# Householder steps with row b summed in PSUM, QL sweeps spread over ten steps, and v.Bv by a scalar-tensor-tensor instruction

## The chip, the cores and the metric

The kernel runs on 1 core of one Trainium2 chip. The metric is the device time of one execution in microseconds (us). Before the change it is 1569.76 us, the median of 3 runs (1568.9 to 1571.31).

## The reference

The input is x (64, 128, 128) and a symmetric normalised adjacency matrix adj (128, 128). Four graph layers follow one another, each as x = x + layer(relu(layernorm(x))). The first layer is spectral: it needs the eigenvectors U of the normalised Laplacian of adj. The others are a two-layer mixing network with batch norm, a two-layer graph convolution with four short LSTMs, and masked attention. The change touches only the eigendecomposition:

```python
deg = jnp.sum(A, axis=0) + jnp.sum(A, axis=1) - jnp.diagonal(A)
d_inv_sqrt = jnp.where(deg > 0, jax.lax.rsqrt(deg), 0.0)
L = jnp.diag(deg) - A
L_norm = d_inv_sqrt[:, None] * L * d_inv_sqrt[None, :]
_, U = jnp.linalg.eigh(L_norm)
agg = jnp.einsum('mn,bnd->bmd', U.T, features)
```

All of it is float32. The signs of the eigenvectors count too, because a relu stands between U.T and U.

## The kernel before, in words

The eigendecomposition comes first and nothing of the four layers runs beside it. All engines run hand-written queues with semaphores between them; `Chain` gives the semaphore by which an engine waits for its own earlier instruction. The stages are:

1. **Tridiagonalisation** (`hh_step`, 126 steps, K=N-2). Step k makes a Householder reflector v from row k of B and updates B by two outer products. Rows are kept as 1 x n tiles on one partition, with n = 127-k columns for the part that is still alive. On VectorE (DVE) a step goes: scalars of the norm (L317 to L323), x0 (L326), Bv (L330), the sum v.Bv (L333, by the custom instruction of the helper in L259, followed by a read of its accumulator), x1 (L335), w (L337), the next row x (L341), the sign of its first element (L310, L311), and B = B + P[3] (L348). ScalarE (ACT) squares and sums the row (L652), takes the root (L654), copies the column out of PSUM (L656), copies row b out of PSUM (L658) and scales v (L660). TensorE (PE) has five float32 products in a step, each run as two passes: the column (L700), row b = row k+1 of B by a column of the identity (L702, after the update of B in L348), the product x.B (L704), and the two outer products (L707, L709). PE issues in program order.
2. **Leaf work beside it.** From step 16 on, implicit QL sweeps run on the top 16 x 16 block of the tridiagonal matrix, to fix the sign of one eigenvector. GpSimd (POOL) does most of it, DVE does the divisions, scans and reductions in short pieces (`leaf_at`), and ACT one square root in a sweep (`leaf_root_of`). A step of the tridiagonalisation has two spots for DVE's pieces: the even one after L326 and before L330, the odd one after L311 and before L348. A sweep takes SPOTS=16 spots, so eight steps. DVE's pieces have 13 instructions in a sweep, at phases 0, 2, 3, 5, 6 and 8. There are 16 sweeps. Steps 16 to 125 hold 220 spots; the rest runs in the next stage.
3. **Sturm counts** (`count_below`, two passes of 63 iterations on DVE, each ending in L448). Every odd iteration of pass 0 has a leaf spot. ACT and PE count signs behind DVE; before that they work through the transposes of the LSTM weights, which are loaded one after the other.
4. **Twisted factorisation** (L486 to L495): 127 iterations on DVE alone, of two reciprocals and two multiply-adds. Then come the eigenvector's entries and sign, the back-transformation and two refinements.
5. The four layers.

## Time and profile before

| what | value |
|---|---|
| median of 3 runs | 1569.76 us |
| profiled execution, its own time | 1570.16 us |
| its span | 1568.5 us |
| tridiagonalisation | 24.7 to 410.9 us |
| Sturm pass 0 / pass 1 | from 427.4 us / from 498.5 us |
| twisted factorisation | 549.3 to 620 us |
| busy share of the span | PE 72%, DVE 67%, ACT 44%, POOL 16% |
| chain that ended last, by engine | PE 50%, DVE 35%, issue 7%, ACT 4% |

Times in the rows are us from the span's start. A row of the timeline has the start, the duration, the engine, the line, the operation, what it writes and reads, shapes and a count; in square brackets stands how long the engine was idle before it and who ended that. L690 is the helper that records nearly all products of this part, and L259 the helper of the custom sum, so these are told apart by tiles. PE's durations include the way through the array: products with single-column weights can start one behind the other before the first one's row ends.

### The profile page before, as it was taken

The numbers are of one execution on the slowest core, as the hardware profiler recorded it, in microseconds if no ns is written. First come the engines' busy times: TensorE is split into PE (matmuls) and PEld (weight loads), VectorE is DVE, ScalarE is ACT, GpSimd is POOL, SyncE is SP. The second block draws the span as 40 slices with busy tenths as digits, with TensorE's granted clock in tenths as the row PEclk, the third lists the DMA queues.
The fourth block names the chain that finished last, engine by engine and source line by source line (L and its number), as shares of the span: only waits on it lengthen the run. The fifth ranks groups of instructions, "written<-read, shape, count | busy, mean of one in ns | idle before, by whom it ended". The sixth has DMA issues, their size and how long they took to land.

```text
span 1568.5 us, 21564 instructions
## 1 busy us (share of the span) xinstructions
PE 1124.1 (72%) x5260; PEld 714.5 (46%) x5260; DVE 1045.5 (67%) x4156; ACT 690.6 (44%) x1760; POOL 253.9 (16%) x900
## 2 busy tenths in 40 slices
PE   3777777776542300448787668999999998589998
PEld 2445555555421200335453356444455443367777
DVE  7777788777889999755576754444343354664766
ACT  2334444444231200024365457675554545365665
POOL 4045555666450000000000000000010020000000
PEclk9999999999975555559898679999999999597999
DMA  4000000000100000000000000000000000000001
GB/s 138 1 1 1 1 1 1 1 1 2 29 21 1 1 0 0 1 0 0 0 0 0 0 0 0 0 0 0 0 0 0 0 0 0 0 15 13 27 20 34
DMA packets 16654, 12.30 MB, mean 8 GB/s; under 512 B 665, under 2 KB 14530, under 8 KB 16578
## 3 DMA queue, kind: packets, MB, share of 16 engines
q1 hardware_dynamic: 16578, 11.49, 2.6%
q8 instruction: 22, 0.36, 0.1%
q14 instruction: 54, 0.44, 0.1%
HBM read 7.23 MB, written 4.19 MB: 7 GB/s over the span
## 4 chain that ended last, share of the span: by engine, by line
PE 50%; DVE 35%; issue 7%; ACT 4%; DVEq 1%; DMA 1%; POOL 1%; ACTq 0%; POOLq 0%
PE P L1343 30%; PE P L690 9%; PE P L1492 4%; DVE B L348 2%; DVE arena L330 2%; DVE arena L444 2%; DVE arena L495 1%; DVE arena L493 1%; DVE scal L320 1%; DVE bst_all L909 1%; ACT hb L1154 1%; DVE arena L448 1%; DVE arena L259 1%; DVE arena L337 1%; PE P L1485 1%
## 5 line engine op out<-in xcount | busy, mean ns | idle before, releaser
L1343 PE MATMUL P<-arena,WT 128*128 (+2 forms) x792 | 329.1, 579 | 3.9 <-ACT L1242 2.9
L1343 PEld LDWEIGHTS P<-arena,WT 128*128 128x128 f32 x792 | 151.8, 192 | 181.1 <-issue 167.3
L690 PE MATMUL P<-arena 1*128 1x127 f32 (+62 forms) x504 | 166.1, 434 | 87.1 <-DVE arena L330 48.6
L1255 ACT ACTIVATE arena<-P,bl 128x512 f32<-128x512 f32 (+1 forms) x252 | 153.3, 636 | 139.5 <-PE P L1343 130.7
L690 PEld LDWEIGHTS P<-arena 1*128 1x128 f32 x504 | 124.1, 307 | 142.4 <-DVE arena L330 112.8
L898 POOL COPY arena<-arena 128x512 f32<-128x512 f32 x16 | 21.5, 1386 | 783.0 <-DVE arena L1075 691.2
L1064 DVE TENSOR_TENSOR arena<-arena 128x512 f32<-128x512 f32 (+1 forms) x36 | 22.0, 610 | 137.4 <-ACT arena L1255 137.4
L652 ACT ACTIVATE arena<-arena 1x127 f32<-1x127 f32 (+62 forms) x126 | 32.2, 256 | 167.5 <-DVE arena L341 157.2
L1154 ACT ACTIVATE hb<-xN,nmr,rsd 128x128 f32 (+1 forms) x192 | 78.5, 481 | 34.9 <-PE P L1343 28.1
L690 PE MATMUL P<-arena,Ib 128*128 128x46 bf16 (+1 forms) x318 | 34.4, 268 | 60.9 <-ACT arena L679 60.4
L195 POOL TENSOR_SCALAR lf<-lf 1x1 f32<-1x1 f32 x210 | 73.3, 349 | 21.9
L1492 PEld LDWEIGHTS P<-arena 128*128 128x128 f32 x512 | 66.6, 200 | 21.5 <-issue 13.2
L1492 PE MATMUL P<-arena 128*128 128x33 f32 x512 | 69.1, 281 | 7.2 <-ACT arena L1300 7.2
L690 PEld LDWEIGHTS P<-I,arena 1*128 1x128 f32 x252 | 66.4, 321 | 4.1 <-DVE arena L305 4.0
L690 PE MATMUL P<-I,arena 1*128 1x1 f32 x252 | 65.0, 325 | 3.2 <-DVE arena L305 3.2
L690 PE MATMUL P<-leaf,ones 1*128 1x1 f32 x2 | 0.6, 342 | 82.5 <-DVE leaf L533 82.5
L690 PE MATMUL P<-B,I 128*1 128x128 f32 (+62 forms) x252 | 47.8, 286 | 11.6 <-DVE B L348 7.6
L690 PEld LDWEIGHTS P<-arena,Ib 128*128 128x128 bf16 x318 | 18.9, 116 | 76.6 <-ACT arena L679 64.1
L690 PE MATMUL P<-B,xcol 128*1 128x128 f32 (+62 forms) x252 | 50.9, 299 | 2.5
L1115 DVE TENSOR_REDUCE mx<-P 128x4 f32<-128x512 f32 x64 | 43.7, 683 | 12.1 <-PE P L1478 12.1
L1062 DVE TENSOR_TENSOR arena<-arena 128x512 f32<-128x512 f32 (+1 forms) x36 | 25.9, 718 | 37.4 <-ACT arena L1255 37.3
L660 ACT ACTIVATE arena<-arena,scal 1x128 f32<-1x128 f32 (+62 forms) x126 | 43.6, 346 | 14.1 <-DVE arena L326 11.4
(477 smaller groups left out, 2451.2 us busy)
## 6 DMA issues: line engine op xcount, KB each, us to landing
out_dram<-xN SPq DMA_DIRECT2D x16, 256.0 KB, 2.3
Wn<-in_L_gnn_Wih_dram SPq DMA_DIRECT2D x4, 256.0 KB, 2.9
Wn<-in_L_gnn_Whh_dram SPq DMA_DIRECT2D x4, 256.0 KB, 2.8
Wqkv<-in_L_gnn_W_dram SPq DMA_DIRECT2D x1, 192.0 KB, 3.6
W1n<-in_L_gnn_W_dram SPq DMA_DIRECT2D x1, 128.0 KB, 4.1
W2n<-in_L_gnn_W_dram SPq DMA_DIRECT2D x1, 128.0 KB, 4.0
Wg<-in_L_gnn_Wg_dram SPq DMA_DIRECT2D x2, 64.0 KB, 3.6
adj<-in_adj_dram SPq DMA_DIRECT2D x1, 64.0 KB, 1.8
```

Of the source, the lines that this page charges most:

```text
L195: l.mark(ts(leaf_p[:,i+1:i+2],leaf_p[:,i:i+1],leaf_x[:,i:i+1],leaf_na[:,i-2:i-1],ALU.mult,ALU.add))
L330: stt(Bv_row[:,k:N],b_row[:,k:N],scal[:,1:2],P[1][0:1,k:N],ALU.mult,ALU.add).then_inc(ev('Bv'),1)
L348: tt(B[:,k+1:N],B[:,k+1:N],P[3][:,k+1:N],ALU.add).then_inc(ev('B_updated'),1)
L444: b=c.mark(tt(seq_d[:,0:2*W],slotS(q),D2[:,i*2*W:(i+1)*2*W],ALU.mult))
L652: a.activation(square_row[:,k+1:N],u[:,k+1:N],ACT.Square,accum_out=scal[:,7:8]).then_inc(ev('column_norm2'),1)
L660: a.activation(v_row[:,k:N],u[:,k:N],ACT.Copy,scale=scal[:,10:11]).then_inc(ev('v_scaled'),1)
L690: def mm(o,l,r,start=True,stop=True): return t.matmul(o,lhsT=l,rhs=r,start=start,stop=stop)
L1115: v.tensor_reduce(s.mx[:,h*4:h*4+4],S3,AX.X,ALU.max).then_inc(ev('attention_max'),1)
L1154: i=a.activation(s.hb[u][:,b*N:(b+1)*N],s.xN[:,bass.ds((2*it+u)*C+b*N,N)],ACT.Relu,bias=s.nmr[:,bass.ds(col,1)],scale=s.rsd[:,bass.ds(col,1)])
L1255: act(s.gt[u][gate][:,0:cols],P[4*u+gate][:,0:cols],f,bias=s.bl[:,4*(p-1)+gate:4*(p-1)+gate+1]).then_inc(ev('lstm_gates'),1)
L1343: def mm(o,l,r,start=True,stop=True,**k): return t.matmul(o,lhsT=l,rhs=r,start=start,stop=stop,**k)
L1492: i=t.matmul(O[:,o:o+33],lhsT=s.pT[h%2][:,b*N:(b+1)*N],rhs=s.vx[u][:,b,h,:],start=True,stop=True)
```

## The change

Three things change.

- **Row b.** It is no longer read from the updated B. In step k, once row b has been copied out, PE starts a sum in P[0] with row k+2 of the B that is not yet updated, adds Bv[k+2] times v, and in the next step adds v[k+2] times w. So P[0] has the updated row without a wait on L348. PE has seven products in a step instead of five; the two new ones have a single element as weights.
- **Leaf sweeps.** A sweep takes 20 spots (ten steps) instead of 16. Seven of DVE's 13 instructions in a sweep go to POOL (multiplications, additions, one comparison, the radicand); six are left, at phases 0, 2 (two), 6, 7 and 10. The 16 sweeps now end in the twisted factorisation: leaf spots stand in both Sturm passes and in iterations up to i=53 of the factorisation. ACT's roots move with them.
- **v.Bv** is a scalar-tensor-tensor with the factor 1.0 and an accumulator output.

```diff
-SPOTS=16
+SPOTS=20
         def rotations(sweep):
-            eng.wait_ge(ev('leaf_from_vector'),5*sweep-1)
+            eng.wait_ge(ev('leaf_from_vector'),5*sweep)
...
-        def new_offdiagonals(sweep):
-            eng.wait_ge(ev('leaf_from_vector'),5*sweep)
-            l(tt(rows(300,20),rows(200,20),rows(240,20),ALU.mult))
-            l(tt(rows(300,20),rows(300,20),rows(142,100),ALU.mult))
-            l(tt(leaf_4e2,row(300,15),row(320,15),ALU.mult))
-            l(ts(leaf_n4,leaf_4e2,-1.0,None,ALU.mult))
+        def new_block(sweep):
+            eng.wait_ge(ev('leaf_from_vector'),5*sweep+1)
+            l(tt(leaf_gamma[:,0:16],leaf_q,leaf_rz,ALU.mult))
+            l.mark(tt(rows(300,20),rows(200,20),rows(240,20),ALU.mult))
+            l.mark(tt(leaf_sums16,leaf_gamma[:,0:16],leaf_gamma[:,1:17],ALU.subtract))
+            l.wait(l.n-1)
+            l.mark(tt(rows(300,20),rows(300,20),rows(142,100),ALU.mult))
+            l.wait(l.n-1)
+            l.mark(ts(leaf_sums16,leaf_sums16,0.5,None,ALU.mult))
+            l.wait(l.n-1)
+            l.mark(tt(leaf_4e2,row(300,15),row(320,15),ALU.mult))
+            l.wait(l.n-1)
+            l.mark(tt(leaf_d[:,0:16],leaf_sums16,leaf_d[:,1:17],ALU.add))
+            l.wait(l.n-1)
+            l.mark(ts(leaf_n4,leaf_4e2,-1.0,None,ALU.mult))
+            l.wait(l.n-1)
+            l(ts(leaf_dd,leaf_d[:,0:15],4*EPS*EPS,None,ALU.mult))
+            l(tt(leaf_dd,leaf_dd,leaf_d[:,1:16],ALU.mult))
         def alive(sweep):
-            if sweep: eng.wait_ge(ev('leaf_from_vector'),5*sweep+1)
...
         def shift(sweep):
             eng.wait_ge(ev('leaf_from_vector'),5*sweep+2)
+            l(ts(leaf_pick,section[0:1,0:15],leaf_idx,None,ALU.is_equal))
             tt(rows(60,20,3),rows(0,20,3),leaf_pick.unsqueeze(1).broadcast_to([1,3,15]),ALU.mult).then_inc(ev('leaf_from_gpsimd'),1)
-            eng.wait_ge(ev('leaf_radicand'),sweep+1)
+            eng.wait_ge(ev('leaf_from_vector'),5*sweep+3)
+            ts(leaf_radicand,leaf_sums[:,0:1],leaf_sums[:,0:1],leaf_sums[:,2:3],ALU.mult,ALU.subtract).then_inc(ev('leaf_radicand'),1)
...
         def shifted(sweep):
-            eng.wait_ge(ev('leaf_from_vector'),5*sweep+3)
+            eng.wait_ge(ev('leaf_from_vector'),5*sweep+4)
+            l(ts(leaf_d[:,16:17],leaf_rden,leaf_sums[:,2:3],leaf_sums[:,1:2],ALU.mult,ALU.add))
...
-            vp=c.mark(ttr(unused_row[:,k+1:N],u[:,k+1:N],Bv_row[:,k+1:N],scal[:,5:6]))
+            vp=c.mark(stt(unused_row[:,k+1:N],u[:,k+1:N],1.0,Bv_row[:,k+1:N],ALU.mult,ALU.mult,accum_out=scal[:,5:6]))
...
-                c(v.reciprocal(leaf_rz,leaf_z[:,0:16]))
-                tt(leaf_gamma[:,0:16],leaf_q,leaf_rz,ALU.mult).then_inc(ev('leaf_from_vector'),1)
-            if phase==3 and sweep:
-                v.wait_ge(ev('leaf_from_vector'),5*sweep)
-                c(tt(leaf_sums16,leaf_gamma[:,0:16],leaf_gamma[:,1:17],ALU.subtract))
-                c(stt(leaf_d[:,0:16],leaf_sums16,0.5,leaf_d[:,1:17],ALU.mult,ALU.add))
-                stt(leaf_dd,leaf_d[:,0:15],4*EPS*EPS,leaf_d[:,1:16],ALU.mult,ALU.mult).then_inc(ev('leaf_from_vector'),1)
-            if phase==5:
+                v.reciprocal(leaf_rz,leaf_z[:,0:16]).then_inc(ev('leaf_from_vector'),1)
+            if phase==6:
                 v.wait_ge(ev('leaf_from_gpsimd'),5*sweep+1)
-                c(v.tensor_reduce(leaf_idx,leaf_hot,AX.X,ALU.max))
-                ts(leaf_pick,section[0:1,0:15],leaf_idx,None,ALU.is_equal).then_inc(ev('leaf_from_vector'),1)
-            if phase==6:
+                v.tensor_reduce(leaf_idx,leaf_hot,AX.X,ALU.max).then_inc(ev('leaf_from_vector'),1)
+            if phase==7:
                 v.wait_ge(ev('leaf_from_gpsimd'),5*sweep+2)
-                c(v.tensor_reduce(leaf_sums,rows(60,20,3),AX.X,ALU.add))
-                stt(leaf_radicand,leaf_sums[:,0:1],leaf_sums[:,0:1],leaf_sums[:,2:3],ALU.mult,ALU.subtract).then_inc(ev('leaf_radicand'),1)
-            if phase==8:
+                v.tensor_reduce(leaf_sums,rows(60,20,3),AX.X,ALU.add).then_inc(ev('leaf_from_vector'),1)
+            if phase==10:
                 v.wait_ge(ev('leaf_from_gpsimd'),5*sweep+3)
-                c(v.reciprocal(leaf_rden,leaf_den))
-                stt(leaf_d[:,16:17],leaf_rden,leaf_sums[:,2:3],leaf_sums[:,1:2],ALU.mult,ALU.add).then_inc(ev('leaf_from_vector'),1)
+                v.reciprocal(leaf_rden,leaf_den).then_inc(ev('leaf_from_vector'),1)
...
-                if pass_==0 and i%2 and HH_SPOTS+i//2<=SPOTS*(SWEEPS-1)+8: leaf_at(HH_SPOTS+i//2)
+                if i%2: leaf_at(HH_SPOTS+HN//2*pass_+i//2)
...
+            if i%2 and HH_SPOTS+HN+i//2<=SPOTS*(SWEEPS-1)+10: leaf_at(HH_SPOTS+HN+i//2)
             c.wait(f)
             f=c.mark(v.reciprocal(inv_down[:,i-1:i],D_down[:,i-1:i]))
...
-            if sweep>=0 and phase==6: leaf_root_of(sweep)
+            if sweep>=0 and phase==8: leaf_root_of(sweep)
...
-                i=2*(SPOTS*sweep+6-HH_SPOTS)+1
-                if h<HALVES and i>0 and i//(SEG//2)==h: leaf_root_of(sweep)
+                root_spot=SPOTS*sweep+8-HH_SPOTS
+                if root_spot>=0 and root_spot//(SEG//4)==h: leaf_root_of(sweep)
...
+        for sweep in range(SWEEPS):
+            if SPOTS*sweep+8-HH_SPOTS>=HN: leaf_root_of(sweep)
...
             mm(P[4][:,0:1],reflector(k),I[0:1,0:1]).then_inc(ev('column_psum'),1)
+            if k: mm(P[0][0:1,k:N],v_row[:,k+1:k+2],w_row[:,k:N],start=False).then_inc(ev('row_b_psum'),1)
             t.wait_ge(ev('B_updated'),k+1)
-            mm(P[0][0:1,k:N],I[:,k+1:k+2],B[:,k:N]).then_inc(ev('row_b_psum'),1)
+            if not k: mm(P[0][0:1,0:N],I[:,1:2],B[:,:]).then_inc(ev('row_b_psum'),1)
             t.wait_ge(ev('column'),k+1)
             mm(P[1][0:1,k:N],xcol[:,:],B[:,k:N]).then_inc(ev('row_xB'),1)
+            t.wait_ge(ev('row_b'),k+1)
+            if k+1<K: mm(P[0][0:1,k+1:N],I[:,k+2:k+3],B[:,k+1:N],stop=False)
             t.wait_ge(ev('Bv'),k+1)
             t.wait_ge(ev('v_scaled'),k+1)
             mm(P[3][:,k+1:N],Bv_row[:,:],v_row[:,k+1:N],stop=False)
+            if k+1<K: mm(P[0][0:1,k+1:N],Bv_row[:,k+2:k+3],v_row[:,k+1:N],start=False,stop=False)
             t.wait_ge(ev('w_row'),k+1)
             mm(P[3][:,k+1:N],v_row[:,:],w_row[:,k+1:N],start=False).then_inc(ev('outer_products'),1)
```

## Rows read from the trace of the kernel before

**Rows 1.** Tridiagonalisation: length; PE, PEld, DVE, ACT, POOL busy (x); PEclk; DMA, GB/s.

```profile
24.70:410.20 385.50, 285.03 (x1252) 206.90 (x1253) 302.59 (x1931) 160.44 (x764) 187.10 (x755) 1.00 0.00 1
```

**Rows 2.** Groups by line, tridiagonalisation: xcount | busy, mean ns | idle before.

```profile
L330 DVE SCALAR_TENSOR_TENSOR arena<-arena,scal,P 1x127 f32<-1x127 f32 (+62 forms) x125 | 32.7, 261 | 11.0 <-PE P L690 9.8
```

**Rows 3.** Timeline, early step, all engines.

```profile
31.05 0.79 PE L690 MATMUL P<-arena 1*128 1x125 f32 x2 [0.50 <-DVE arena L330]
32.00 0.78 PE L690 MATMUL P<-arena 1*128 1x125 f32 x2 [0.16 <-DVE arena L337]
33.23 0.58 PE L690 MATMUL P<-B,I 128*1 128x125 f32 x2 [0.21 <-DVE B L348]
33.60 0.62 PE L690 MATMUL P<-B,xcol 128*1 128x125 f32 x2
33.74 0.15 DVE L326 TENSOR_TENSOR arena<-arena,scal 1x1 f32<-1x1 f32 x1
34.33 0.33 DVE L330 SCALAR_TENSOR_TENSOR arena<-arena,scal,P 1x125 f32<-1x125 f32 x1 [0.43 <-PE P L690]
```

**Rows 4.** Timeline of DVE, a step in the middle.

```profile
207.81 0.28 DVE L330 SCALAR_TENSOR_TENSOR arena<-arena,scal,P 1x74 f32<-1x74 f32 x1
208.23 0.22 DVE L259 CUSTOM_DVE_ANT_0 arena<-arena 1x73 f32<-1x73 f32 x1
208.39 0.07 DVE L259 DVE_READ_ACCUMULATOR2_ANT scal<- 1x1 f32 x1
208.39 0.28 DVE L335 SCALAR_TENSOR_TENSOR arena<-arena 1x72 f32<-1x72 f32 x1
208.59 0.28 DVE L337 SCALAR_TENSOR_TENSOR arena<-arena,scal 1x73 f32<-1x73 f32 x1
208.97 0.28 DVE L341 SCALAR_TENSOR_TENSOR arena<-arena 1x72 f32<-1x72 f32 x1
```

**Rows 5.** Groups by line: scalar-tensor-tensor on one element, immediate or pointer.

```profile
L311 DVE SCALAR_TENSOR_TENSOR scal<-arena 1x1 f32<-1x1 f32 x125 | 17.2, 138 | 0.0
L386 DVE SCALAR_TENSOR_TENSOR lf<-lf 1x1 f32<-1x1 f32 x14 | 2.9, 206 | 0.5
```

**Rows 6.** Timeline, L341 alone, a middle and a late sweep.

```profile
236.34 0.27 DVE L341 SCALAR_TENSOR_TENSOR arena<-arena 1x63 f32<-1x63 f32 x1
257.30 0.27 DVE L341 SCALAR_TENSOR_TENSOR arena<-arena 1x56 f32<-1x56 f32 x1
260.09 0.28 DVE L341 SCALAR_TENSOR_TENSOR arena<-arena 1x55 f32<-1x55 f32 x1
...
351.21 0.24 DVE L341 SCALAR_TENSOR_TENSOR arena<-arena 1x23 f32<-1x23 f32 x1
353.74 0.23 DVE L341 SCALAR_TENSOR_TENSOR arena<-arena 1x22 f32<-1x22 f32 x1
356.81 0.23 DVE L341 SCALAR_TENSOR_TENSOR arena<-arena 1x21 f32<-1x21 f32 x1
370.38 0.22 DVE L341 SCALAR_TENSOR_TENSOR arena<-arena 1x16 f32<-1x16 f32 x1
372.87 0.22 DVE L341 SCALAR_TENSOR_TENSOR arena<-arena 1x15 f32<-1x15 f32 x1
```

**Rows 7.** One line each: min/median/max ns, first to last start.

```profile
L448 DVE TENSOR_TENSOR arena<-arena x63: 178/246/290, 427.4 to 480.4; 128x92 f32<-128x92 f32 x63
L448 DVE TENSOR_TENSOR arena<-arena x63: 245/247/256, 498.5 to 544.3; 128x92 f32<-128x92 f32 x63
L493 DVE TENSOR_SCALAR arena<-neg_off,arena x127: 262/265/273, 549.3 to 619.9; 128x1 f32<-128x1 f32 x127
```

**Rows 8.** Timeline of Sturm pass 0: ACT, then DVE.

```profile
447.37 0.48 ACT L670 ACTIVATE arena<-P 128x368 bf16<-128x368 f32 x1
448.67 0.28 ACT L648 ACTIVATE lf<-lf 1x1 f32<-1x1 f32 x1
449.76 0.15 DVE L385 RECIPROCAL lf<-lf 1x1 f32<-1x1 f32 x1 [2.31 <-POOL lf L226]
```

More of the change, by code:

```diff
@@ L246, in _ @@
                 rotations(sweep)
-                new_offdiagonals(sweep)
+                new_block(sweep)
             alive(sweep)
```

## The prediction

> **What bounds the kernel now.** I read the page first, for the stages: the change touches only the eigendecomposition, and the layers behind it start when it ends, so a microsecond saved there is one of the time. Then the busy times by stage, then the groups by line, and then the timeline of single steps. In the tridiagonalisation DVE is busy 302.59 of 385.50 us and PE 285.03, at the full clock of 1.00 [rows 1]. Neither is full: a step is a ring of short instructions that hand over to each other, and the reader is to look for who starts last at each handover.
>
> Three handovers matter. (1) Bv (L330) waits for the product x.B. In an early step that product starts at 33.60, right behind the product for row b, which starts at 33.23, as soon as B is updated; L330 starts at 34.33 after 0.43 us idle that PE ended [rows 3]. Over all steps L330's engine is idle 11.0 us before it, 9.8 of them by PE [rows 2]; in the middle step at 74 columns its row shows no idle time [rows 4]. (2) From L330 to L341 DVE works in its own order: L330 starts at 207.81, the custom sum at 208.23, x1 at 208.39, w at 208.59, the next row at 208.97 [rows 4]. Each is on the ring. (3) DVE's leaf pieces stand in the same queue ahead of L330 or of L348. What they cost is the excess of a sweep's steps over free ones. In the middle, the eight steps from 236.34 to 260.09 take 23.75 us; a free step there takes 2.79 (257.30 to 260.09), and as steps shrink with the columns the mean over the eight would be about 2.84, so 22.7: excess 1.05. Late, 351.21 to 372.87 is 21.66 us against eight times about 2.52 (the free one at the end is 2.49): excess 1.5. The piece with scan, reciprocal and product is the dearest: 3.07 for its step (353.74 to 356.81) against 2.52, while the lone reciprocal's step takes 2.53 [rows 6].
>
> **Row b.** The product of 125 columns leaves its place between the update of B and x.B, so x.B can start up to 0.37 us earlier (33.23 for 33.60) [rows 3]. The 0.43 us that DVE is idle leave room for it. The third part of the new sum now stands before x.B, but right behind the column's product, where PE waits for L348 and for the copied column anyway: it is one more product of the same column count with a gap ahead of x.B, so I cost it at nothing; if that cover is gone, it takes back up to the same 0.37. The gain goes to zero where L330 no longer waits for PE, at some 62 to 74 columns [rows 4]. A triangle of 0.36 us over 62 steps is 11 us, which agrees with the 9.8 us of idle time plus what lies hidden in leaf steps [rows 2].
>
> PE has two more products. Row k+2 of the old B goes between x.B's end and the outer products, where PE waits about half a microsecond for Bv; nothing. The product Bv[k+2] times v goes between the two outer products. In the early step these start at 31.05 and 32.00, and the first one's row ends at 31.84 [rows 3]. The inserted one occupies PE about as long as the gap between two single-weight products, 0.37 us at 125 columns; part of it overlaps the first one's tail. I take a delay of the second outer product of 0.05 to 0.1 us for the first 27 steps and none later: 2 us. That delay is on the path, since L348 follows the second outer product and DVE's scalars stand behind L348 in the queue. The bounds for this term are 0 and 0.2 us in every step, as below. Row b nets 11 - 2 = **9 us**.
>
> **Leaf pieces.** Before, the tridiagonalisation holds 220/16 = 13.75 sweeps; at 1.05 each (early ones less, late ones up to 1.5) 14.4 us. After, 11 sweeps with six instructions each. From the late sweep: the lone reciprocal costs about 0; scan plus reciprocal without the product 0.55 less 0.2, so 0.35; a reduction before L330 0.1, a reduction before L348 (where DVE waits for PE) nothing, the reciprocal of one element 0.05: 0.5 a sweep, 5.5 us. Gain **9 us**. What it needs is that POOL keeps up: it is busy 187.10 us for 13.75 sweeps [rows 1], 13.6 a sweep; seven more instructions of 0.2 to 0.3 us make about 15.5, with waits perhaps 19, in ten steps of at least 24.9 us (2.49 each [rows 6]).
>
> The rest of the leaf work moves to later stages. Pass 0 takes 53.0 us (427.4 to 480.4), pass 1, without leaf pieces, 45.8 [rows 7]. Of the 7.2 us, 2.3 are one stall for ACT's root [rows 8]; 4.9 are 26 instructions, so 0.19 each. After, pass 0 has 12 instructions (2.3 us), pass 1 nine (1.7), the twisted factorisation nine (1.7; it is DVE alone, 0.56 us an iteration [rows 7]). The stall gets longer: ACT can take the root only when it has done the weights' copies and the first sign groups. In the new order the root stands behind the group at 447.37 instead of the one before 448.67, so it starts at about 447.8, and DVE goes on as long after it as now, 1.09 us (448.67 to 449.76 [rows 8]): at 448.9. But DVE now wants it at i=21 instead of i=25. It is there at 427.4 + 20 x 0.74 (45.8/62) + 0.9 for four pieces = 443.1. Stall 5.8 for 2.3. Sum behind the tridiagonalisation: 2.3 + 1.7 + 1.7 + 5.8 - 7.2 = **4.3 us lost**.
>
> **v.Bv.** The trace of before has no such instruction with an accumulator. The custom one starts 0.14 us after L330's end (207.81 + 0.28 to 208.23), where L341 starts 0.10 after L337's (208.59 + 0.28 to 208.97): 0.04 that may go. From the custom one to x1 are 0.16 us, with the accumulator's read (0.07) beside x1. A plain scalar-tensor-tensor of the same length holds the queue 0.20 (208.39 to 208.59) [rows 4], but it takes its scalar by a pointer; with an immediate it is 0.07 shorter on one element (138 against 206 ns) [rows 5]. So from 0.07 shorter (0.04 + 0.16 - 0.13) to 0.07 longer (0.20 + 0.07 - 0.16 - 0.04): -9 to +9 us over 126 steps. Both forms near it have the immediate's price, but the read may cost; I take -0.02 a step, **2.5 us gained**.
>
> A page speaks against this part. In the rows, a plain scalar-tensor-tensor takes 0.33 us for 125 columns and 0.28 for 74 [rows 3, 4], 1.0 ns a column, so it is not halved by two float32 inputs in SBUF. The Trainium skill's page "Vector Engine (DVE) Microarchitecture Reference", section "Points that are easy to get wrong", says that this form with two non-bf16 SBUF sources halves throughput, since no port is left for the accumulator's readback. The rows contradict it without an accumulator; with one no row here shows it. By that rule the sum would come out as in rival 3.
>
> **Sum.** 1570.16 (the profiled execution's own time, 1.7 above its span and 0.4 above the median of the runs) - 9 - 9 - 2.5 + 4.3 = **1554 us**.
>
> **Rivals.**
> 1. *PE's queue becomes the bound (slower).* The inserted product delays the second outer product in every step, and with it L348, the scalars and the next column. For it: the early outer products leave only 0.16 us idle between them [rows 3]. Against it: with fewer columns the inserted product shrinks at 3 ns a column while DVE's chain from Bv to w shrinks at half of that. It decides from 0.13 us a step (16/126). At 0.2 us, a fourth of the early outer product's 0.79 [rows 3], the cost is 25 us: 1554 + 25 = 1579. Chance 9%.
> 2. *Row b brings nothing*, since the third part takes the place of the product removed. 1554 + 9 = 1563. For it: same column count, still ahead of x.B in an in-order queue. Against it: the wait for L348 between them. Chance 11%.
> 3. *The accumulator form is dear.* Without halving, +9 for -2.5: 1565.5, chance 12%. With 1.0 ns more for each of 64 columns on average, another 8 us: 1573.5, chance 4%.
> 4. *POOL or the root holds DVE up*, about 1 us in each of 16 sweeps: 1570. For it: the stall at 449.76. Chance 5%. That the change doesn't do what it says has no weight of its own: the removed instructions are plain in the diff.
>
> The forecast has the remaining 59%. Its own range is 1547 to 1560. The range for 8 in 10 takes in the term v.Bv from -9 to +9, a leaf gain of 12, and rivals 2 and 3 without halving: 1544 to 1567. A difference under 0.2% (3 us) is no change for a measurement of this kernel. Faster is the forecast, rival 2, and rival 3 without halving: 0.82. Rival 4 is the same, with a part of rival 3: 0.06. Slower: rival 1 and the halving: 0.12.
>
> **What would show it.** In the early step L330 should start some 0.3 us earlier after the update of B, with x.B starting right behind the update; steps of 60 columns and less without leaf pieces should be as long as now, but for v.Bv. The tridiagonalisation should end 20 us earlier. A sweep's excess should be 0.5 us in ten steps. The reciprocal of phase 10 in pass 0 should wait about 6 us for POOL. The prediction is wrong if the second outer product starts more than 0.1 us after w in middle steps, if x1 starts later than 0.2 us after the sum, or if a reduction waits for POOL in most sweeps.

## The result, and the profile after

The changed kernel takes 1573.7 us (median of 12 runs, 1571.33 to 1590.61) against 1568.93 us before (12 runs, 1567.56 to 1571.31). The ratio is 1.0048, with a 95% interval of 1.0028 to 1.0069: about 5 us slower, where 1554 us was forecast. Of the 12 runs of the changed kernel eight lie between 1571.3 and 1574.2 us, three between 1581.4 and 1582.4, and one at 1590.6; the profile below is of the one at 1581.65.

The busy times by stage of the changed kernel, columns as in [rows 1]: the tridiagonalisation, from its end to the eigenvectors, and the layers behind.

```profile
24.70:421.90 397.20, 350.44 (x1751) 220.82 (x1749) 288.85 (x1819) 161.55 (x761) 176.06 (x705) 1.00 0.01 1
421.90:704.40 282.50, 74.32 (x484) 46.39 (x483) 243.24 (x1233) 36.15 (x81) 92.53 (x294) 0.57 0.03 7
704.40:1579.80 875.40, 758.54 (x3512) 458.89 (x3512) 480.48 (x949) 492.21 (x910) 21.18 (x16) 0.92 0.02 5
```

The first row answers to [rows 1]. DVE is busy 288.85 us for 302.59: the leaf work did leave. But the stage is 11.7 us longer (397.20 for 385.50), and PE has 499 more matmul records and 65 us more busy time. The second stage is 2.9 us longer (279.6 before). The third is 3.3 us shorter (878.70 before), though the change touches nothing in it.

Where the 11.7 us sit is in DVE's groups by line of the same stage (L344 is Bv, before L330; L362 the update of B, before L348; L347 v.Bv):

```profile
L344 DVE SCALAR_TENSOR_TENSOR arena<-arena,scal,P 1x127 f32<-1x127 f32 (+62 forms) x125 | 32.7, 262 | 10.7 <-PE P L698 3.9 <-DVE wide L368 0.2
L362 DVE TENSOR_TENSOR B<-B,P 128x127 f32<-128x127 f32 (+62 forms) x125 | 27.8, 223 | 54.8 <-PE P L698 54.8
L347 DVE SCALAR_TENSOR_TENSOR arena<-arena 1x126 f32<-1x126 f32 (+62 forms) x125 | 27.0, 216 | 14.3 <-DVE arena L344 0.5
L347 DVE DVE_READ_ACCUMULATOR arena<-arena 1x1 f32 x125 | 8.8, 71 | 0.0
```

Before Bv, the idle time put down to PE fell from 9.8 us [rows 2] to 3.9, but all idle time there only from 11.0 to 10.7: the short gaps, put down to nobody, have grown. Before the update of B, DVE is idle 54.8 us, all of it until PE's outer products; the same line of before reads:

```profile
L348 DVE TENSOR_TENSOR B<-B,P 128x127 f32<-128x127 f32 (+62 forms) x125 | 27.5, 220 | 21.9 <-PE P L690 21.7
```

So 33 us of new waiting stand at one handover. With row b as before and the other two parts in place (e1 below) the wait there is 28.1 us: 6 of the 33 come from the work taken off DVE, 27 from row b. An early step of the changed kernel shows how; it answers to [rows 3] and the steps around it (start, us, engine, line, operation, idle time before):

```profile
35.42 0.33 DVE L351 SCALAR_TENSOR_TENSOR arena<-arena,scal 1x124 f32<-1x124 f32 x1
35.60 0.08 PEld L698 LDWEIGHTS P<-arena 1*1 1x1 f32 x2 [0.22 <-issue]
36.10 0.50 PEld L698 LDWEIGHTS P<-arena 1*128 1x128 f32 x2 [0.42 <-DVE arena L351]
...
36.99 0.28 DVE L362 TENSOR_TENSOR B<-B,P 128x124 f32<-128x124 f32 x1 [0.56 <-PE P L698]
...
37.04 0.57 PE L698 MATMUL P<-arena 1*1 1x124 f32 x2
...
37.54 0.57 PE L698 MATMUL P<-B,xcol 128*1 128x124 f32 x2
...
38.22 0.33 DVE L344 SCALAR_TENSOR_TENSOR arena<-arena,scal,P 1x124 f32<-1x124 f32 x1 [0.22 <-PE P L698]
```

w (L351) is ready at 35.75, but the second outer product's weights load only at 36.10: 0.35 us later. Between the two outer products stands the single-element product, whose weights load at 35.60. In a middle step it is the same:

```profile
205.98 0.28 DVE L351 SCALAR_TENSOR_TENSOR arena<-arena,scal 1x75 f32<-1x75 f32 x1
...
206.54 0.50 PEld L698 LDWEIGHTS P<-arena 1*128 1x128 f32 x2 [0.25 <-DVE arena L351]
...
207.35 0.23 DVE L362 TENSOR_TENSOR B<-B,P 128x75 f32<-128x75 f32 x1 [0.45 <-PE P L698]
...
208.42 0.28 DVE L344 SCALAR_TENSOR_TENSOR arena<-arena,scal,P 1x75 f32<-1x75 f32 x1
...
208.81 0.24 DVE L347 SCALAR_TENSOR_TENSOR arena<-arena 1x74 f32<-1x74 f32 x1
...
208.99 0.07 DVE L347 DVE_READ_ACCUMULATOR arena<-arena 1x1 f32 x1
208.99 0.28 DVE L349 SCALAR_TENSOR_TENSOR arena<-arena 1x73 f32<-1x73 f32 x1
```

w ends at 206.26 and the weights load at 206.54, 0.28 us later.

For the rest it helps to cut each step in three, by the starts on DVE: Bv to w, w to the update of B, the update to the next Bv. Summed over all steps, from each kernel's trace (us):

| kernel | Bv to w | w to update | update to Bv: first 45 steps | next 40 | last 40 |
|---|---|---|---|---|---|
| before | 97.7 | 144.2 | 59.3 | 44.6 | 41.8 |
| after | 93.7 | **169.6** | 52.5 | 42.8 | 40.5 |
| after, row b as before (e1) | 92.8 | 142.9 | 58.2 | 41.1 | 38.1 |
| leaf part alone (e3) | 97.2 | 142.5 | 58.3 | 41.1 | 38.1 |
| v.Bv alone (e4) | 93.8 | 144.5 | 59.2 | 44.6 | 41.9 |
| row b alone (e2) | 98.5 | 164.5 | 54.1 | 45.6 | 43.1 |

### The profile page after: what moved, and what is told of

It is laid out like the page before. It is cut to its first block, busy times and chain, and to the rows that moved or that the text cites. A ratio compares the mean times of both kernels' runs of the same rounds, so it can differ in the third digit from the quotient of the medians.

```text
span 1579.8 us, 22704 instructions
## 1 busy us (share of the span) xinstructions
PE 1188.3 (75%) x5760; PEld 728.6 (46%) x5760; DVE 1032.8 (65%) x4048; ACT 692.8 (44%) x1760; POOL 306.4 (19%) x1038
## 4 chain that ended last, share of the span: by engine, by line
PE 57%; DVE 29%; issue 6%; ACT 5%; DVEq 1%; DMA 1%; ACTq 0%; POOL 0%; POOLq 0%
PE P L1355 29%; PE P L698 17%; PE P L1504 3%; DVE arena L449 2%; DVE bst_all L921 2%; DVE arena L499 1%; DVE arena L501 1%; DVE scal L334 1%; ACT hb L1166 1%; ACT arena L666 1%; DVE arena L453 1%; DVE arena L344 1%; DVE arena L447 1%; PE P L1497 1%; PE P L1463 1%
## 5 line engine op out<-in xcount | busy, mean ns | idle before, releaser
L698 PE MATMUL P<-arena 1*128 1x127 f32 (+62 forms) x1004 | 245.2, 356 | 36.6 <-ACT arena L666 24.3
L1267 ACT ACTIVATE arena<-P,bl 128x512 f32<-128x512 f32 (+1 forms) x252 | 153.5, 636 | 137.4 <-PE P L1355 130.0
L698 PEld LDWEIGHTS P<-arena 1*128 1x128 f32 x1004 | 145.0, 191 | 115.0 <-DVE arena L344 69.5
L1166 ACT ACTIVATE hb<-xN,nmr,rsd 128x128 f32 (+1 forms) x192 | 78.5, 481 | 34.8 <-PE P L1355 28.1
L195 POOL TENSOR_SCALAR lf<-lf 1x1 f32<-1x1 f32 x210 | 85.6, 408 | 21.9
L362 DVE TENSOR_TENSOR B<-B,P 128x127 f32<-128x127 f32 (+62 forms) x126 | 28.0, 222 | 55.4 <-PE P L698 55.4
L698 PE MATMUL P<-B,xcol 128*1 128x128 f32 (+62 forms) x252 | 47.7, 286 | 10.1 <-ACT xcol L662 6.6
```

The costliest lines, as they stand in the source:

```text
L195: l.mark(ts(leaf_p[:,i+1:i+2],leaf_p[:,i:i+1],leaf_x[:,i:i+1],leaf_na[:,i-2:i-1],ALU.mult,ALU.add))
L362: tt(B[:,k+1:N],B[:,k+1:N],P[3][:,k+1:N],ALU.add).then_inc(ev('B_updated'),1)
L698: def mm(o,l,r,start=True,stop=True): return t.matmul(o,lhsT=l,rhs=r,start=start,stop=stop)
L1166: i=a.activation(s.hb[u][:,b*N:(b+1)*N],s.xN[:,bass.ds((2*it+u)*C+b*N,N)],ACT.Relu,bias=s.nmr[:,bass.ds(col,1)],scale=s.rsd[:,bass.ds(col,1)])
L1267: act(s.gt[u][gate][:,0:cols],P[4*u+gate][:,0:cols],f,bias=s.bl[:,4*(p-1)+gate:4*(p-1)+gate+1]).then_inc(ev('lstm_gates'),1)
```

## The experiments

Theory D (delay): the product put between the outer products holds back the second one in every step. Its rival in the tridiagonalisation: what is lost lies in the leaf part or the accumulator form. Theory P (position): what the layers take depends on when they start.

**e1: the change without row b.**

```diff
-            if k: mm(P[0][0:1,k:N],v_row[:,k+1:k+2],w_row[:,k:N],start=False).then_inc(ev('row_b_psum'),1)
...
+            mm(P[0][0:1,k:N],I[:,k+1:k+2],B[:,k:N]).then_inc(ev('row_b_psum'),1)
...
-            if k+1<K: mm(P[0][0:1,k+1:N],I[:,k+2:k+3],B[:,k+1:N],stop=False)
...
-            if k+1<K: mm(P[0][0:1,k+1:N],Bv_row[:,k+2:k+3],v_row[:,k+1:N],start=False,stop=False)
```

> The changed kernel with the products of row b as before (five a step). Theory D (the two single-element products delay PE): steps of 75 columns without leaf pieces fall from 3.2 us to 2.95, the tridiagonalisation ends before 402 us, and the time is 1559 to 1564, some 12 us under the changed kernel. Rival L (the leaf sweeps over ten steps cost what was lost, through POOL): steps stay near 3.2 us and the time stays at 1570 or more.

Measured: 1547.05 us (4 runs, 1546.19 to 1547.84), ratio to before 0.9868 [0.9851, 0.9884]. The row-b part alone turns a gain of 1.3% into a loss of 0.5%. It is also 12 us below the expected range, and that mixes two things. Against the changed kernel, whose layers take 867.4 us in its second profile (e12) and e1's 865.4, nearly all of the difference is in the tridiagonalisation: 26.1 us, where some 12 were expected. Against before, the layers are 13.3 us shorter (865.4 for 878.7), which no expectation had. The busy times of its tridiagonalisation and the group of the update of B:

```profile
24.80:395.90 371.10, 280.96 (x1253) 205.54 (x1253) 287.30 (x1819) 158.39 (x761) 176.90 (x705) 1.00 0.00 1
```

```profile
L362 DVE TENSOR_TENSOR B<-B,P 128x127 f32<-128x127 f32 (+62 forms) x125 | 27.8, 222 | 28.1 <-PE P L698 26.5
```

The stage is 26.1 us shorter than after's, and the wait before the update 26.7 us shorter (54.8 to 28.1): in sum the whole difference is that handover. The gain and the loss from the update to Bv nearly cancel (135.8 us in after, 137.4 in e1). One middle step of e1 for the 206.54 above:

```profile
195.18 0.28 DVE L351 SCALAR_TENSOR_TENSOR arena<-arena,scal 1x76 f32<-1x76 f32 x1
...
195.51 0.49 PEld L698 LDWEIGHTS P<-arena 1*128 1x128 f32 x2 [0.23 <-DVE arena L351]
...
196.33 0.23 DVE L362 TENSOR_TENSOR B<-B,P 128x76 f32<-128x76 f32 x1 [0.24 <-PE P L698]
```

The weights load 0.05 us after w's end (195.46), not 0.28, and the update starts 1.15 us after w's start, not 1.37.

**e2: row b alone, on the kernel before.** The same four products as above, put into before.

```diff
+            if k: mm(P[0][0:1,k:N],v_row[:,k+1:k+2],w_row[:,k:N],start=False).then_inc(ev('row_b_psum'),1)
...
-            mm(P[0][0:1,k:N],I[:,k+1:k+2],B[:,k:N]).then_inc(ev('row_b_psum'),1)
+            if not k: mm(P[0][0:1,0:N],I[:,1:2],B[:,:]).then_inc(ev('row_b_psum'),1)
...
+            if k+1<K: mm(P[0][0:1,k+1:N],I[:,k+2:k+3],B[:,k+1:N],stop=False)
...
+            if k+1<K: mm(P[0][0:1,k+1:N],Bv_row[:,k+2:k+3],v_row[:,k+1:N],start=False,stop=False)
```

> The kernel before with only the new sum of row b. Theory D: the second outer product starts 0.3 us later after w than before in steps of every length, steps of 75 columns take about 3.2 us, and the time is 1577 to 1583. Rival L: steps up to 62 columns gain up to 0.3 us and the time is about 1560.

Measured: 1587.05 us (1585.75 to 1601.54), ratio 1.0147 [1.0095, 1.0199]. That is 4 us above the expected range. Its tridiagonalisation takes 403.8 us, 18.3 more than before. On top of the leaf part and the accumulator form it costs 26.1 (397.2 against 371.1). From w to the update it adds 20.3 us to before and 26.7 to e1: where before has leaf pieces ahead of L348, DVE comes late anyway and PE's delay is hidden (from w to the update 1.37 us before and 1.38 in e2, at 102 columns), and after has fewer of those.

**e3: the leaf part alone** (e1 with v.Bv by the custom instruction).

```diff
-            vp=c.mark(stt(unused_row[:,k+1:N],u[:,k+1:N],1.0,Bv_row[:,k+1:N],ALU.mult,ALU.mult,accum_out=scal[:,5:6]))
+            vp=c.mark(ttr(unused_row[:,k+1:N],u[:,k+1:N],Bv_row[:,k+1:N],scal[:,5:6]))
```

> The kernel before with only the leaf sweeps over ten steps. Theory D: a sweep's excess over free steps falls from 1.05 us to 0.5, 9 us are gained in the tridiagonalisation and 3 to 4 lost behind it: 1562 to 1565. Rival L: 1572 or more, with DVE's reductions waiting for POOL.

Measured: 1550.75 us (1549.97 to 1558.97), 0.9907 [0.9878, 0.9935]. Tridiagonalisation 375.1 us, 10.4 shorter. The time is 11 us below the expected range, by the layers (865.3 us for 878.7).

**e4: v.Bv alone, on the kernel before.**

```diff
-            vp=c.mark(ttr(unused_row[:,k+1:N],u[:,k+1:N],Bv_row[:,k+1:N],scal[:,5:6]))
+            vp=c.mark(stt(unused_row[:,k+1:N],u[:,k+1:N],1.0,Bv_row[:,k+1:N],ALU.mult,ALU.mult,accum_out=scal[:,5:6]))
```

> The kernel before with only v.Bv by the scalar-tensor-tensor instruction with accumulator. From the changed kernel's trace it starts 0.03 us sooner after Bv and x1 starts 0.02 us later after it: 0 to 2 us gained, 1567 to 1569. The rival that it is dear: 1575 or more.

Measured: 1564.88 us (10 runs, 1563.78 to 1566.64), 0.9977 [0.9968, 0.9987]. Tridiagonalisation 382.1 us, 3.4 shorter; of the table's three segments only Bv to w changed (97.7 to 93.8). The expectation, 0 to 2 us gained, was too low: it had x1 start later behind the sum, and it doesn't (0.16 us in the mean over steps in both). The rival that the accumulator form is dear is out.

**e5 and e6: an idle product between the outer products.** Both are e1 with one product whose result nobody reads. Its moving side has one column, so it streams next to nothing; its weights have one element in e5 and 128 in e6, as the outer products' have. If any further instruction costs, both are slow; if the change of the weights' shape does, only e5.

```diff
+            mm(P[6][0:1,0:1],Bv_row[:,k+1:k+2],v_row[:,k+1:k+2])
```

```diff
+            mm(P[6][:,0:1],Bv_row[:,:],v_row[:,k+1:k+2])
```

> The changed kernel with row b as before, and one idle product added between the outer products: weights of one element and one moving column, into an unused bank; its result is not used. Theory D (what costs is the change of the weights' shape, on which PE waits until the product before has left the array): the second outer product starts 0.25 to 0.3 us later after w in steps of all lengths, and the time is 25 to 35 us over the same kernel without it (1547): 1572 to 1582. Rival Q (what costs is the columns that the inserted products stream): one column costs nothing, 1547 to 1550.

> As the last one, but the idle product has all 128 elements of the row as weights, the outer products' own shape, and again one moving column. Theory D: no wait for the array, but two loads of 128 columns, 0.2 us each; they fit between the outer products where those are long (75 columns and more), and delay the second one by up to 0.4 us at 17 columns: 1555 to 1565, with early steps unchanged. Rival Q: 1547 to 1550.

Measured: e5 1558.47 us (10 runs, 1556.5 to 1573.34), 0.9942 [0.9913, 0.9971], tridiagonalisation 382.2; e6 1573.76 (1570.64 to 1586.76), 1.0027 [0.9992, 1.0061], tridiagonalisation 395.5. Both expectations were missed: e5 lies between theory D's 1572 to 1582 and rival Q's 1547 to 1550, and e6, meant as the cheap one, is the dearer. Late steps say why; DVE's next row (L355) at 17 and 16 columns in e1, e5 and e6:

```profile
355.52 0.22 DVE L355 SCALAR_TENSOR_TENSOR arena<-arena 1x17 f32<-1x17 f32 x1
358.01 0.22 DVE L355 SCALAR_TENSOR_TENSOR arena<-arena 1x16 f32<-1x16 f32 x1
```

```profile
363.42 0.22 DVE L355 SCALAR_TENSOR_TENSOR arena<-arena 1x17 f32<-1x17 f32 x1
366.13 0.22 DVE L355 SCALAR_TENSOR_TENSOR arena<-arena 1x16 f32<-1x16 f32 x1
```

```profile
373.19 0.22 DVE L355 SCALAR_TENSOR_TENSOR arena<-arena 1x17 f32<-1x17 f32 x1
376.10 0.22 DVE L355 SCALAR_TENSOR_TENSOR arena<-arena 1x16 f32<-1x16 f32 x1
```

A step takes 2.49, 2.71 and 2.91 us. In early steps neither costs anything: w to update sums to 55.2, 55.3 and 55.9 us over the first 45 steps, since the idle product is through before w is there. So a change of shape alone is free where there is time for it; in after the inserted product streams its 124 columns as well. Late, the gap between the first outer product and w closes, and both delay the second: 42.8, 50.2 and 58.3 us over the last 41. In e6's late steps the loads of 128 weights follow each other at 0.21 us a pass, whatever is moved, so the wide product is the dearer one there. An inserted product thus costs in two ways, by its loads and by its shape, and this pair doesn't separate them. e9 does.

**e9: row b with wide weights.** The three products take all elements from k+2 on (126-k of them) as weights, and use one row of the result.

```diff
...
-            if k+1<K: mm(P[0][0:1,k+1:N],Bv_row[:,k+2:k+3],v_row[:,k+1:N],start=False,stop=False)
+            if k+1<K: mm(P[0][0:K-k,k+1:N],Bv_row[:,k+2:N],v_row[:,k+1:N],start=False,stop=False)
```

> The changed kernel with wide weights in the sum: the products take all elements from k+2 on, 126-k of them, as weights, so rows k+2 to 127 of the update stand in P[0] and row k+2 is the first. While there are over 64 of them the shape is that of the outer products. Theory D: until step 62 steps are 0.1 to 0.2 us shorter than in the changed kernel, and from there they are as long as in it: 1560 to 1570. Rival Q: no difference, 1573.

Measured: 1564.88 us (10 runs, 1563.37 to 1573.33), 0.9972 [0.9948, 0.9996], against 1.0048 for the changed kernel: the same sums in the same order, with larger loads, and 9 us less. w to update takes 56.0 us over the first 45 steps, against 66.8 in after and 55.2 in e1. Then, within one step, the gain is gone; the next rows of e9 from 66 down to 63 columns, which is also the number of the inserted product's weights in that step:

```profile
221.13 0.27 DVE L355 SCALAR_TENSOR_TENSOR arena<-arena 1x66 f32<-1x66 f32 x1
224.07 0.27 DVE L355 SCALAR_TENSOR_TENSOR arena<-arena 1x65 f32<-1x65 f32 x1
227.01 0.27 DVE L355 SCALAR_TENSOR_TENSOR arena<-arena 1x64 f32<-1x64 f32 x1
230.27 0.27 DVE L355 SCALAR_TENSOR_TENSOR arena<-arena 1x63 f32<-1x63 f32 x1
```

2.94 us a step twice, then 3.26, of which about 0.2 are a leaf piece that e1 has at the same place (2.84, then 3.03). From w to the update no leaf piece mixes in; here it is in the steps with 65 and with 64 weights:

```profile
223.70 0.27 DVE L351 SCALAR_TENSOR_TENSOR arena<-arena,scal 1x66 f32<-1x66 f32 x1
...
224.81 0.23 DVE L362 TENSOR_TENSOR B<-B,P 128x66 f32<-128x66 f32 x1 [0.23 <-PE P L698]
...
226.63 0.28 DVE L351 SCALAR_TENSOR_TENSOR arena<-arena,scal 1x65 f32<-1x65 f32 x1
...
228.07 0.22 DVE L362 TENSOR_TENSOR B<-B,P 128x65 f32<-128x65 f32 x1 [0.52 <-PE P L698]
```

1.11 us, then 1.44; e1 has 1.12 in both. The single records of PE show where it goes. With 65 weights the inserted product's load starts 0.11 us after the second pass of the first outer product, and the next outer product's load 0.11 us after the inserted one's second pass. With 64 it is 0.35 and 0.24 us. One column fewer can't cost that by its size: from 64 weights on, PE treats the inserted product as another shape than the 128 of the outer products. This is a threshold, not a slope, and it is what tells the change of shape from the loads. At 32 weights there is no second jump (0.33 us at 33 and at 32).

The Trainium skill's page "TensorEngine Tiling (Array Packing)", section "Key Properties", says: "Changing tiling mode (not just tile) drains the TensorE". The jump of e9 at 64 weights agrees with it, if a product of 64 weights or fewer runs in another mode than one of 128; no run here shows the mode itself. What the traces do show is the drain: at all 375 places in after where a product with one weight stands next to an outer or a column's product with 128, the load starts no sooner than 0.07 us before the recorded end of the product before it, while behind a product of the same shape it starts 0.2 to 0.4 us before that end.

**e7: no single-element product.** It leaves out both products that carry the update, so row b is that of the B before the update: of the three products the one that reads I and B keeps its place behind x.B.

```diff
-            if k: mm(P[0][0:1,k:N],v_row[:,k+1:k+2],w_row[:,k:N],start=False).then_inc(ev('row_b_psum'),1)
...
-            if k+1<K: mm(P[0][0:1,k+1:N],Bv_row[:,k+2:k+3],v_row[:,k+1:N],start=False,stop=False)
```

> The changed kernel without both single-element products: row b is the row of B before the update (its output is wrong by that). It shows what taking the update out of row b's path is worth by itself. The prediction put that at 11 us, mostly in steps over 75 columns: against 1547 without the sum of row b, 1536 to 1540, with steps of 124 columns at 3.3 us and steps of 75 and less as in the kernel with row b as before. If theory D is wrong and the early product with the old B costs, it stays over 1550.

Measured: 1547.64 us (4 runs, 1543.71 to 1561.87), 0.9866 [0.9793, 0.9938]; tridiagonalisation 368.3 us. That is 2.7 us below e1, where some 10 were expected. Update to Bv in e7 is 51.5 us over the first 45 steps, against 58.2 in e1: 6.7 gained. Then it is 42.9 and 40.5 against 41.1 and 38.1: 4.2 lost. An early step of e7 shows the limit of the gain:

```profile
35.56 0.28 DVE L362 TENSOR_TENSOR B<-B,P 128x124 f32<-128x124 f32 x1 [0.27 <-PE P L698]
36.04 0.57 PE L698 MATMUL P<-B,xcol 128*1 128x124 f32 x2 [0.35 <-ACT xcol L662]
...
36.72 0.33 DVE L344 SCALAR_TENSOR_TENSOR arena<-arena,scal,P 1x124 f32<-1x124 f32 x1
```

Update to Bv is 1.16 us here, 1.23 in after (36.99 to 38.22), 1.43 in e1. With row b out of the way x.B waits for ACT's copy of the column: at most 0.27 us are to be had, not 0.37. The loss in later steps is a slower start of x.B: its weights load 0.11 us after the column's copy ends when PE has nothing before it (348.27 to 348.38 in e7), and 0.06 us when the row-b product has just run (349.00 to 349.06 in e1). Why was not tried.

**e8: the root earlier.** e1, with ACT's root of pass 0 put ahead of the last copy of the LSTM weights instead of behind a sign group.

```diff
-                if root_spot>=0 and root_spot//(SEG//4)==h: leaf_root_of(sweep)
+                if sweep>HH_SPOTS//SPOTS and root_spot//(SEG//4)==h: leaf_root_of(sweep)
...
+        if q==7: before_last()
```

> The changed kernel with row b as before (1547) and ACT's root for the sweep that starts in Sturm pass 0 taken before the last copy of the LSTM weights instead of behind the first sign groups. From the stall of the reciprocal of phase 10, 5 to 6 us come off pass 0: 1541 to 1543, if the clock in the layers stays as it is. If the sign groups set the end of the pass instead, 1546 to 1547.

Measured: 1541.43 us (4 runs, 1541.08 to 1541.85), 0.9824 [0.9808, 0.9841]. The changed kernel's reciprocal of phase 10 in pass 0, then the same one in e8 with its root:

```profile
459.94 0.15 DVE L391 RECIPROCAL lf<-lf 1x1 f32<-1x1 f32 x1 [5.69 <-POOL lf L239]
```

```profile
425.49 0.28 ACT L654 ACTIVATE lf<-lf 1x1 f32<-1x1 f32 x1
...
428.38 0.14 DVE L391 RECIPROCAL lf<-lf 1x1 f32<-1x1 f32 x1
```

The stall of 5.69 us (forecast 5.8) is gone, and pass 0 takes 47.5 us for e1's 53.9, as expected.

**e10: before, with 3 us more ahead of the layers.** One DVE instruction on a scratch area between pass 1 and the twisted factorisation.

```diff
+        c(tt(arena2[:,0:2900],arena2[:,0:2900],arena2[:,2900:5800],ALU.max))
```

> The kernel before with one idle DVE instruction of about 3 us between Sturm pass 1 and the twisted factorisation. All kernels so far with the leaf sweeps over ten steps are 3 us longer between the tridiagonalisation and U, and 10 to 13 us shorter in the layers, which no edit touches, by fewer stretches at half clock. Theory P (the position of TensorE's half-clock stretches against the work does it, and 3 us move it): the layers take 865 us instead of 878 and the time falls to 1558 to 1562. Rival X (something else in the leaf change does it): 1572.

Measured: 1572.52 us (11 runs, 1570.6 to 1585.76), 1.0018 [1.0008, 1.0027], 3.4 us more than before: the inserted time (2.9 us in its trace) and hardly more. Theory P is not borne out by it. Its profile is of its slowest run, 1585.76 us, with 891.2 us in the layers.

**e11: the best of the parts.** e8, with e9's wide row b in the steps below 60 alone (more than 64 weights).

```diff
+            if k and wide_k: mm(P[0][0:K-k+1,k:N],v_row[:,k+1:N],w_row[:,k:N],start=False).then_inc(ev('row_b_psum'),1)
...
+            if not (k and wide_k): mm(P[0][0:1,k:N],I[:,k+1:k+2],B[:,k:N]).then_inc(ev('row_b_psum'),1)
```

> As e8_root_early, and row b summed in PSUM with wide weights (over 64 of them) in steps 1 to 59 only, as before in the others. By theory D no shape changes between the outer products and about 0.03 us a step are gained from the earlier row b: 1 to 3 us under e8_root_early. If the wide products cost what the idle wide one cost in late steps, it is up to 5 us over it.

Measured: 1540.8 us (4 runs, 1539.32 to 1541.19), 0.9816 [0.98, 0.9833], tridiagonalisation 369.8 for e1's 371.1. w to update is within 0.8 us of e1 in all three thirds (56.0, 44.9 and 42.8 against 55.2, 45.0 and 42.8), and update to Bv is 2.5 us shorter in the first. It beats both kernels, but all except 0.6 us of that is e8's.

**e12: the changed kernel, once more.** No edit. The first profiled execution of it took 1581.65 us, above its median of 1573.7.

> The changed kernel itself once more. Its runs fell into two groups, near 1573 and near 1581. If that is the clock in the layers, a run near 1573 has the same tridiagonalisation (about 397 us) and 8 us less behind U, with a higher mean clock.

Measured: 1573.04 us (10 runs, 1571.58 to 1574.12), 1.0024 [1.0015, 1.0034]. Its tridiagonalisation and its layers:

```profile
24.60:421.80 397.20, 350.47 (x1750) 220.68 (x1749) 288.74 (x1819) 161.46 (x761) 175.99 (x705) 1.00 0.01 2
704.30:1571.70 867.40, 751.40 (x3512) 452.74 (x3512) 480.66 (x949) 492.16 (x910) 21.26 (x16) 0.93 0.02 5
```

The tridiagonalisation is the same to 0.1 us (397.20 twice): its account holds. The layers take 867.40 us, 8 less than in the first profile. So the two runs of one program differ by 8 us, all of it there.

## Why the prediction was wrong

**The failed step is the product between the two outer products** ("a delay of 0.05 to 0.1 us for the first 27 steps and none later: 2 us"). It cost 26.7 us from w to the update (169.6 against 142.9). The product itself is dearer than the 0.37 us that I took, but shrinks as I took it: from its load to the next outer product's load are 0.50 us at 124 columns, 0.33 at 75, 0.23 at 42 and 0.14 at 17, some 3.3 ns a column. What I left out is the wait ahead of it. Its weights load only 0.34 us after the first outer product's second pass has started, at 124 columns as at 75, and still 0.30 at 17; a product of the outer products' own shape follows after 0.07 to 0.15. Both together are 0.84 us at 124 columns, 0.68 at 75, 0.57 at 42 and 0.44 at 17, while w is ready after 0.49, 0.39, 0.28 and 0.20 us; and the gap of 0.16 us between the outer products in [rows 3] doesn't hold them. The second outer product's load came 0.28 us after w in the mean over steps, for 0.06 before: 0.35 us in the early step above, 0.28 in the middle one, 0.23 at 17 columns. That is rival 1, which I gave 9%; its price at 0.2 us a step is what the runs show (0.21 us a step, 27 us). My argument against it, that the product shrinks at 3 ns a column, was true and beside the point, since the wait ahead of it hardly shrinks. The 1579 of rival 1 count the first 2 us of delay twice, which the 1554 already hold; 1577 would follow. Of the prediction's own signs of being wrong this one came: the second outer product more than 0.1 us after w in middle steps.

[Rows 3] did not show the wait: no product there has single-element weights. The trace of before did, at another place. Between the column's product (weights 1 x 128) and that of row b (128 x 1) the shape changes too, and the load of row b never comes sooner than 0.275 us after the column's second pass; in 14 of 126 steps it comes just then. In the early step the wait for L348 hides it. The prediction named "0 and 0.2 us in every step" as bounds of this term, but the upper one was not carried into the range of the time.

That the time is 1573.7 us and not near 1583.5 (before with 11.7 and 2.9 us more) is luck: the layers took less, which nothing in the prediction foresaw. That rival 3 with halving gave 1573.5 is chance too, since e4 rules it out.

**Row b's gain** was put at 11 us and is 5.7 in the first 45 steps (58.2 against 52.5 us from update to Bv), of which 4.1 are lost again in the later ones (42.8 and 40.5 against 41.1 and 38.1). The direction was right and the price too high, for two reasons: ACT's copy of the column ends next, so 0.27 us at most are to be had (e7), and the third product takes 0.07 of those, its own change of shape standing ahead of x.B (1.23 against 1.16 us). So rival 2, the third part in place of the product removed, holds for a part. Even e7, which leaves the small products out, gains only 2.6 us from update to Bv over all steps.

**Leaf pieces:** 9 us forecast in the tridiagonalisation, 10.4 measured alone (e3). The reductions and the lone reciprocals are as cheap as taken from [rows 6]. POOL kept up: before none of the groups of leaf pieces did DVE wait more than 0.3 us in all, over ten or eleven sweeps.

**v.Bv:** 2.5 us forecast, 3.4 in the stage and 3.9 from Bv to w (e4), and by the ratio 3.6 us of 1568.7. Of the two sources I named, only the start was there: the sum starts 0.114 us after Bv's end in the mean instead of 0.148, and x1 0.16 us after the sum as before, with the accumulator's read (0.07) beside it (208.81 and 208.99 above are a step with 0.18). The Trainium skill's page "Vector Engine (DVE) Microarchitecture Reference", section "Points that are easy to get wrong", has this form at halved throughput with two non-bf16 sources in SBUF. As the prediction took it, at some 1 ns more a column, it doesn't hold here with an accumulator either: 0.24 us for 74 columns and 0.28 for 123, 0.8 ns a column, hardly more than the custom instruction's 0.22 for 73 and 0.28 for 125. If the rule is meant against a faster form, no run here tests it.

**Behind the tridiagonalisation:** 4.3 us forecast, 2.9 measured. The pass rows, answering to [rows 7], and the stall of 5.69 us agree with the working; pass 0 takes 53.3 us, pass 1 47.3 and the factorisation 71.5:

```profile
L453 DVE TENSOR_TENSOR arena<-arena x63: 178/247/295, 439.1 to 492.4; 128x92 f32<-128x92 f32 x63
L453 DVE TENSOR_TENSOR arena<-arena x63: 177/247/295, 510.5 to 557.8; 128x92 f32<-128x92 f32 x63
L499 DVE TENSOR_SCALAR arena<-neg_off,arena x127: 262/265/275, 562.9 to 634.4; 128x1 f32<-128x1 f32 x127
```

Against 53.0, 45.8 and 70.6 this is 0.3, 1.5 and 0.9: 2.7 us. The nine pieces in pass 1 cost 0.17 us each and the nine in the factorisation 0.10, for 0.19 forecast; pass 0 grew by 0.3 us where 0.9 were forecast.

**The layers** were taken as unchanged. They aren't, though no instruction of them differs: 878.7 us before, 865.3 in e3, 865.4 in e1, 876.8 in e4, 878.5 in e2, 867.4 and 875.4 in the two profiles of after. This is why the loss in the medians is 5 us and not 14.6 (11.7 + 2.9), and why e3 beat its expectation. What one sees is the granted clock. The time that the layers run at the level of 1.2 GHz, summed from each trace's record of the clock:

| kernel | layers, us | of that at half clock | layers less half of that |
|---|---|---|---|
| before | 878.7 | 141 | 808 |
| row b alone (e2) | 878.5 | 145 | 806 |
| after, first profile | 875.4 | 138 | 806 |
| after, second (e12) | 867.4 | 127 | 804 |
| e1 | 865.4 | 121 | 805 |
| e10, slowest run | 891.2 | 174 | 804 |

The last column is 802 to 809 us in all fourteen traces: the half clock accounts for nearly all of the spread. In two stretches of the attention stage of before it is 0.50, for 10 us each, behind 11 us in which PE was busy 10.33 us at the full level; in e1 the stretches at the same distance behind the eigenvectors stay at 1.00, though PE is as busy (columns as in [rows 1]):

```profile
1400.00:1411.00 11.00, 10.33 (x96) 8.06 (x95) 7.24 (x15) 7.12 (x15) 0.00 (x0) 0.99 0.09 26
1411.00:1421.00 10.00, 10.00 (x35) 7.59 (x35) 2.51 (x6) 4.91 (x10) 0.00 (x0) 0.50 0.00 0
1438.00:1448.00 10.00, 10.00 (x37) 7.93 (x37) 2.82 (x6) 4.79 (x10) 0.00 (x0) 0.50 0.00 0
```

```profile
1400.00:1411.00 11.00, 10.66 (x101) 8.53 (x99) 7.86 (x15) 7.78 (x15) 0.00 (x0) 1.00 0.08 24
1427.00:1437.00 10.00, 9.66 (x72) 7.64 (x74) 7.03 (x14) 7.40 (x15) 0.00 (x0) 1.00 0.09 26
```

At 0.50, PE gets through 35 and 37 matmuls in 10 us, at 1.00 through 72 and more: each stretch costs about half its length, and the two together 10 of the 13 us between the kernels. What decides over them stays open. It isn't the start of the layers alone: kernels without the leaf change keep 877 to 879 us with starts 17.9 us later (e2) and 3.6 earlier (e4), and e10's median fits the same with a start 3 later. Those with it show 865 to 869, except 875.4 in e6 and in the first profile of after; and after's second profile has 867.4 from the same start (704.3 for 704.4).

## What to carry to other kernels

A product with few weights between two with many is not free because it is small: look in the trace at the distance from one product's last pass to the next one's load where the shapes differ, and at what waits behind in PE's queue. Such a place may exist before the change, hidden behind another wait. In a ring of handovers, count an inserted instruction at the handover that it stands before, with its bound in every step, and carry that bound into the range. Work taken off an engine shows only as far as the other engine of the ring leaves it: the same row-b part cost 18 us before the other two parts and 26 behind them.

## What the runs showed of the hardware

- Across a change of the weights' shape on PE, the next load starts 0.34 us after the start of the second pass of an outer product with 128 weights (0.30 at 17 columns). Behind a single-element product it is 0.34 us at 124 columns, 0.26 at 75, 0.11 at 17, and 0.09 with one column (e5). In each case that is 0.07 us before the recorded end of the product, which is modelled. Products of the same shape follow sooner (before: 0.07 us from the second outer product's second pass to the column's weights in early steps, 0.15 in late ones).
- The limit lies at 64 weights (e9): 65 and more follow as 128 do, and 64 take 0.33 us more from w to the update (1.44 for 1.11). The same product costs 0.18 us at 17 columns (1.21 against e1's 1.03).
- A product with one moving column and 128 weights delays the next one by up to 0.4 us a step late in the stage (2.91 against 2.49 us): its two loads, 0.21 us apart (e6), are the cost.
- The custom instruction starts 0.033 us later behind its producer than the built-in one with accumulator (0.148 against 0.115 us in the mean, before and e4).
- The same instructions of the layers take 865 to 891 us in kernels whose layers don't differ, and 8 us more or less in two profiles of one program, with 121 to 174 us of them at half the clock.
